# Experts of layer 0: hidden values in two halves with a PSUM bank each, token rows copied by ScalarE and VectorE, and both up-products ahead of both down-products

## The reference

```
logits = x_flat @ W_router
topk_p, topk_i = jax.lax.top_k(jax.nn.softmax(logits, axis=-1), 2)
topk_p = topk_p / topk_p.sum(axis=-1, keepdims=True)
...
for e in range(E):                       # 8 experts, 128 -> 512 -> 128
    h = jax.nn.relu(x_flat @ W1[e] + b1[e])
    out = out + combine[:, e:e + 1] * (h @ W2[e] + b2[e])
```

## Time and profile before

| what | value |
|---|---|
| median of 3 runs | 1411.34 us (1411.24 to 1416.61) |
| the profiled execution's own time | 1410.25 us |
| its span, first to last instruction | 1408.4 us |
| TensorE busy | 1103.4 us, 78% |
| VectorE busy | 825.5 us, 59% |
| ScalarE busy | 744.3 us, 53% |
| GpSimd busy | 546.3 us, 39% |
| experts of layer 0 (first to last residual, line 921) | from 451.3 to 943.2 us |

### The profile page before, as it was taken

How to read it: one execution, slowest core, us unless ns; L and a number is a source line. 1 busy time by engine, 2 the same in 40 slices (tenths; PEclk the granted TensorE clock), 3 DMA queues, 4 the chain that set the end, 5 groups by cost and what they waited for, 6 DMA issues and landing times. The chain is left out here.

```text
span 1408.4 us, 32619 instructions
## 1 busy us (share of the span) xinstructions
PE 1103.4 (78%) x9950; PEld 731.9 (52%) x9951; DVE 825.5 (59%) x1640; ACT 744.3 (53%) x1748; POOL 546.3 (39%) x401
## 2 busy tenths in 40 slices
PE   6869787665602999999999989965999999965586
PEld 2324344332302988888888888862444444422354
DVE  3653345443525555555555555542899999984576
ACT  5855397655711555555555555544666666622364
POOL 0000006555570322322322222232799999991000
PEclk9989899888755999999999999998999999985599
DMA  6100001331122111111111111112111111101000
GB/s 202 47 1 0 1 1 54 112 129 52 33 67 62 44 39 37 38 38 37 37 38 38 38 37 37 38 31 82 30 30 60 60 60 60 46 30 77 0 1 30
DMA packets 60525, 65.22 MB, mean 46 GB/s; under 512 B 9841, under 2 KB 50301, under 8 KB 60336
## 3 DMA queue, kind: packets, MB, share of 16 engines
q1 hardware_dynamic: 49616, 46.47, 11.3%
q0 software_dynamic: 8832, 17.00, 3.7%
q10 hardware_dynamic: 2016, 0.94, 0.2%
HBM read 37.12 MB, written 28.55 MB: 47 GB/s over the span
## 5 line engine op out<-in xcount | busy, mean ns | idle before, releaser
L921 DVE SCALAR_TENSOR_TENSOR m_hl<-ps,m_hh 128x512 f16<-128x512 f32 x292 | 200.4, 686 | 158.2 <-ACT m_hh L893 155.9
L801 POOL DMA_INDIRECT expert_out<-m_result,m_token x148 | 144.5, 976 | 377.8 <-DVE m_result L933 374.1
L893 ACT ACTIVATE m_hh<-ps 128x512 f16<-128x512 f32 x292 | 174.2, 596 | 179.0 <-PE ps L854 176.7
L836 PE MATMUL ps<-m_x,weights 128*128 128x128 f16 x1168 | 212.8, 221 | 44.5 <-ACT m_x L887 43.7
L838 PE MATMUL ps<-m_x,weights 128*128 128x128 f16 x1168 | 211.7, 220 | 0.0
L837 PE MATMUL ps<-m_x,weights 128*128 128x128 f16 x1168 | 211.7, 220 | 0.0
L745 POOL DMA_INDIRECT dispatched<-d_rows,slot x128 | 128.4, 1003 | 211.6 <-DVE slot L647 126.2
L851 PE MATMUL ps<-weights,m_hh 128*128 128x128 f16 x1160 | 209.2, 219 | 0.0
L853 PE MATMUL ps<-weights,m_hl 128*128 128x128 f16 x1160 | 209.2, 219 | 0.0
L852 PE MATMUL ps<-weights,m_hh 128*128 128x128 f16 x1160 | 209.2, 219 | 0.0
L1043 POOL TENSOR_TENSOR iv_pool_sum<-iv_pool_sum,iv_pool_part 128x1024 f32<-128x1024 f32 x80 | 188.6, 2358 | 12.1 <-DVE iv_pool_part L1258 3.8
(11 more groups left out here) (306 smaller groups left out, 2238.0 us busy)
## 6 DMA issues: line engine op xcount, KB each, us to landing
m_rows<-dispatched SPq DMA_DIRECT2D x152, 65.5 KB
X<-x SPq DMA_DIRECT2D x16, 512.0 KB, 4.3
iv_got<-expert_out SPq DMA_DIRECT2D x16, 512.0 KB, 4.3
out<-X SPq DMA_DIRECT2D x16, 512.0 KB, 3.0
Y<-w_moe SPq DMA_DIRECT2D x8, 512.0 KB
expert_out<-m_result,m_token POOLq DMA_INDIRECT x148, 2.2
dispatched<-d_rows,slot POOLq DMA_INDIRECT x128
Y<-w_last SPq DMA_DIRECT2D x1, 2048.0 KB
```

The source lines that it names most:

```text
L801: pool.indirect_dma_start(env.yt, bass.IndirectOffsetOnAxis(ap=token[:, k:k + 1], axis=0), result[:, k, :], None, bounds_check=TOKENS - 1, ...
L836: pe.matmul(out, high, xh, start=True, stop=False)
L893: act.activation(hh[e][:, :], hidden[e], ACT.Relu).then_inc(hi_ready[e], 1)
L921: dve.scalar_tensor_tensor(hl[e][:, :], hidden[e], 0.0, hh[e][:, :], ALU.max, ALU.subtract).then_inc(h_split[e], 1)
```

## The change

- `hidden[e]` becomes two tensors of 256 columns, each in a bank of its own; `high` and `low` become two instructions each, of 256 columns, with a count of their own (`h_ready`, `hi_ready`, `h_split` now count halves). `up` waits for `h_split` twice, at m = 0 and m = 2, and announces each half. `down` announces `y_ready` twice: after its block k = 1, when the first half of `hh[e]` and `hl[e]` is read, and at its end. `down` itself waits for both halves of `h_split`.
- `take` is split: ScalarE copies the high half (127 x 128), VectorE the low half, from a bank each. `up` and `turn_rows` have one more wait (`xl_ready`), and in `up` the product with the low values comes last of the three.
- TensorE's order in a tile becomes `up(i+1, 0)`, `up(i+1, 1)`, `turn_rows(i+2)`, `down(i, 0)`, `down(i, 1)`. ScalarE's: `take(i+2)`, `high(i+1, 0)` twice, `part`, `high(i+1, 1)` twice. VectorE's: `take(i+2)`, four `low`, token copy, `result`.
- The four semaphores of `wait_apart` become one.

The diff, without those of its places that only put `env.passed` for `env.passed["..."]`:

```diff
--- before.py
+++ after.py
@@ -756,7 +756,7 @@
         sem = lambda n: ctx.enter_context(nc.semaphore(n))
         sb = lambda n, s, d=F32: ctx.enter_context(nc.sbuf_tensor(n, s, d))
         landed = [sem(f"m0_landed{k}") for k in range(RING // 2)]
-        rows_ready, turned, x_ready = sem("m0_rows_ready"), sem("m0_turned"), sem("m0_x_ready")
+        rows_ready, turned, x_ready, xl_ready = sem("m0_rows_ready"), sem("m0_turned"), sem("m0_x_ready"), sem("m0_xl_ready")
         h_ready, hi_ready, h_split, y_ready = ([sem(f"m0_{n}{e}") for e in range(2)] for n in ("h_ready", "hi_ready", "h_split", "y_ready"))
         part_ready, out_ready, result_free = (sem(f"m0_{n}") for n in ("part_ready", "out_ready", "result_free"))
         stored, ready = [sem(f"m0_stored{k}") for k in range(OUTS)], sem("m0_ready")
@@ -767,9 +767,10 @@
         xh, xl = x[:, 0, :], x[:, 1, :]
         hh, hl = ([sb(f"m0_{n}{e}", [P, H0], F16) for e in range(2)] for n in ("hh", "hl"))
         part, result, token = sb("m0_part", [P, C]), sb("m0_result", [P, OUTS, C]), sb("m0_token", [P, OUTS], U32)
-        hidden = [env.psum[0][:, e * HALF:(e + 1) * HALF] for e in range(2)]
-        y = [env.psum[1][:, e * HALF:e * HALF + C] for e in range(2)]
-        turn = env.psum[2][:, 0:2 * P]
+        hidden = [[env.psum[e][:, h * HALF:h * HALF + H0 // 2] for h in range(2)] for e in range(2)]
+        y = [env.psum[2][:, e * HALF:e * HALF + C] for e in range(2)]
+        turn = [env.psum[3][:, k * HALF:k * HALF + P] for k in range(2)]
+        part_cols = [slice(h * H0 // 2, (h + 1) * H0 // 2) for h in range(2)]
         at = lambda i: bass.ds(i % RING, 1)
         gate = lambda i, g: rows[:, at(i), C + g:C + g + 1].rearrange("p k c -> p (k c)")
         count = lambda engine, k, low, high: engine.value_load(env.totals[0:1, k:k + 1], min_val=low, max_val=high)
@@ -797,7 +798,7 @@
             pool.sem_inc(result_free, 2)
 
             def send(j, k):
-                wait_apart(pool, out_ready, j * OUTS + k + RING + 1, env.passed["pool"])
+                wait_apart(pool, out_ready, j * OUTS + k + RING + 1, env.passed)
                 pool.indirect_dma_start(env.yt, bass.IndirectOffsetOnAxis(ap=token[:, k:k + 1], axis=0), result[:, k, :], None,
                                         bounds_check=TOKENS - 1, oob_is_err=False).then_inc(stored[k], 16)
                 if k >= 2:
@@ -821,26 +822,31 @@
             def turn_rows(i):
                 pe.wait_ge(rows_ready, i + 1)
                 pe.wait_ge(x_ready, i + 1)
+                pe.wait_ge(xl_ready, i + 1)
                 for part_ in range(2):
-                    mm = pe.matmul(turn[:, part_ * P:(part_ + 1) * P],
+                    mm = pe.matmul(turn[part_],
                                    halves[:, at(i), part_ * C:(part_ + 1) * C].rearrange("p k c -> p (k c)"), idh[:, :], start=True, stop=True)
                 mm.then_inc(turned, 1)
 
             def up(i, e, expert):
                 w = W[:, expert * WCOLS:(expert + 1) * WCOLS]
                 pe.wait_ge(x_ready, i + 2)
-                pe.wait_ge(h_split[e], i + 1)
                 for m in range(KM):
-                    out = hidden[e][:, m * P:(m + 1) * P]
+                    if m % 2 == 0:
+                        pe.wait_ge(h_split[e], i * 2 + m // 2 + 1)
+                    out = hidden[e][m // 2][:, m % 2 * P:(m % 2 + 1) * P]
                     high, low = w[:, m * P:(m + 1) * P], w[:, H0 + m * P:H0 + (m + 1) * P]
                     pe.matmul(out, high, xh, start=True, stop=False)
-                    pe.matmul(out, high, xl, start=False, stop=False)
-                    mm = pe.matmul(out, low, xh, start=False, stop=True)
-                mm.then_inc(h_ready[e], 1)
+                    pe.matmul(out, low, xh, start=False, stop=False)
+                    if m == 0:
+                        pe.wait_ge(xl_ready, i + 2)
+                    mm = pe.matmul(out, high, xl, start=False, stop=True)
+                    if m % 2 == 1:
+                        mm.then_inc(h_ready[e], 1)
 
             def down(i, e, expert):
                 w = W[:, expert * WCOLS:(expert + 1) * WCOLS]
-                pe.wait_ge(h_split[e], i + 2)
+                pe.wait_ge(h_split[e], i * 2 + 4)
                 if e == 0:
                     pe.wait_ge(part_ready, i + 1)
                 else:
@@ -850,14 +856,16 @@
                     high, low = w[:, 2 * H0 + k * P:2 * H0 + (k + 1) * P], w[:, 3 * H0 + k * P:3 * H0 + (k + 1) * P]
                     pe.matmul(y[e], hh[e][:, cols], high, start=(k == 0), stop=False)
                     pe.matmul(y[e], hh[e][:, cols], low, start=False, stop=False)
-                    pe.matmul(y[e], hl[e][:, cols], high, start=False, stop=False)
+                    mm = pe.matmul(y[e], hl[e][:, cols], high, start=False, stop=False)
+                    if k == 1:
+                        mm.then_inc(y_ready[e], 1)
                 pe.matmul(y[e], env.ones16[:, :], w[:, 4 * H0:4 * H0 + C].bitcast(BF16), start=False, stop=True).then_inc(y_ready[e], 1)
 
             def tile(i, pair, following):
                 up(i + 1, 0, following[0])
+                up(i + 1, 1, following[1])
+                turn_rows(i + 2)
                 down(i, 0, pair[0])
-                turn_rows(i + 2)
-                up(i + 1, 1, following[1])
                 down(i, 1, pair[1])
 
             pe.wait_ge(ready, 3)
@@ -883,14 +891,15 @@
             def take(i):
                 act.wait_ge(turned, i + 1)
                 if not isinstance(i, int) or i > 0:
-                    act.wait_ge(h_ready[1], i)
-                act.activation(x[0:C - 1, :, :], turn[0:C - 1, :].rearrange("p (h s) -> p h s", h=2), ACT.Copy).then_inc(x_ready, 1)
+                    act.wait_ge(h_ready[1], i * 2)
+                act.activation(xh[0:C - 1, :], turn[0][0:C - 1, :], ACT.Copy).then_inc(x_ready, 1)
 
             def high(i, e):
-                act.wait_ge(h_ready[e], i + 1)
-                if not isinstance(i, int) or i > 0:
-                    act.wait_ge(y_ready[e], i)
-                act.activation(hh[e][:, :], hidden[e], ACT.Relu).then_inc(hi_ready[e], 1)
+                for h in range(2):
+                    act.wait_ge(h_ready[e], i * 2 + h + 1)
+                    if not isinstance(i, int) or i > 0:
+                        act.wait_ge(y_ready[e], i * 2 - 1 + h)
+                    act.activation(hh[e][:, part_cols[h]], hidden[e][h], ACT.Relu).then_inc(hi_ready[e], 1)
 
             act.wait_ge(ready, 3)
             act.sem_inc(x_ready, 1)
@@ -900,11 +909,11 @@
             take(1)
             total = count(act, 0, PAIRS, MAX_TILES)
             with act.Fori(0, total) as i:
+                take(i + 2)
                 high(i + 1, 0)
-                act.wait_ge(y_ready[0], i + 1)
+                act.wait_ge(y_ready[0], i * 2 + 2)
                 act.wait_ge(out_ready, i + RING)
                 act.activation(part[:, :], y[0], ACT.Copy, scale=gate(i, 0)).then_inc(part_ready, 1)
-                take(i + 2)
                 high(i + 1, 1)
 
         @block.vector
@@ -913,26 +922,41 @@
             dve.memset(x[96:P, 0, :], 1.0).then_inc(ready, 1)
             dve.memset(x[96:P, 1, :], 0.0).then_inc(ready, 1)
             for e in range(2):
-                dve.sem_inc(h_split[e], 1)
+                dve.sem_inc(h_split[e], 2)
             dve.sem_inc(out_ready, RING)
-
-            def low(i, e):
-                dve.wait_ge(hi_ready[e], i + 1)
-                dve.scalar_tensor_tensor(hl[e][:, :], hidden[e], 0.0, hh[e][:, :], ALU.max, ALU.subtract).then_inc(h_split[e], 1)
-
-            low(0, 0)
-            low(0, 1)
+            dve.wait_ge(ready, 3)
+            dve.sem_inc(xl_ready, 1)
+
+            def take(i):
+                dve.wait_ge(turned, i + 1)
+                if not isinstance(i, int) or i > 0:
+                    dve.wait_ge(h_ready[1], i * 2)
+                dve.tensor_copy(xl[0:C - 1, :], turn[1][0:C - 1, :]).then_inc(xl_ready, 1)
+
+            def low(i, e, h):
+                cols = part_cols[h]
+                dve.wait_ge(hi_ready[e], i * 2 + h + 1)
+                dve.scalar_tensor_tensor(hl[e][:, cols], hidden[e][h], 0.0, hh[e][:, cols], ALU.max, ALU.subtract).then_inc(h_split[e], 1)
+
+            take(0)
+            for e in range(2):
+                for h in range(2):
+                    low(0, e, h)
+            take(1)
             total = count(dve, 0, PAIRS, MAX_TILES)
             with dve.Fori(0, total) as i:
-                low(i + 1, 0)
-                dve.wait_ge(y_ready[1], i + 1)
+                take(i + 2)
+                low(i + 1, 0, 0)
+                low(i + 1, 0, 1)
+                low(i + 1, 1, 0)
+                low(i + 1, 1, 1)
+                dve.wait_ge(y_ready[1], i * 2 + 2)
                 dve.wait_ge(part_ready, i + 2)
                 dve.wait_ge(result_free, i + 1)
                 out = bass.ds(i % OUTS, 1)
```

(13 more changed lines are left out.)

## The result

The changed kernel takes 1474.47 us (median of four runs, 1470.47 to 1475.94) against 1411.29 (1410.61 to 1416.61) for the kernel before beside it: ratio 1.0435, 95% interval 1.0402 to 1.0467. The profiled execution took 1475.94, of which 1474.0 are the span.

What follows compares the result with a forecast made beforehand. It took the experts' stage as bounded by TensorE's 2.90 us of products plus a 0.48 wait per step. A held loop of 3.72 against 3.38 over 145 steps gave +49 us: 1460 us, range 1396 to 1481.

Steps and rivals of the forecast that it cites:

- the held loop: Experts' step looping through GpSimd's indirect DMA, ReLU, residual, token copy and `result`: 3.72 us a step, 1460 us, chance 0.65.
- Token copy 0.47 behind the residual: On VectorE, the token copy starts 0.47 us after the last residual's start, between 0.33 and 0.60.
- DMA to ReLU 1.43: ReLU of expert 1's second half starts 1.43 us after the indirect DMA's start, because TensorE's announcement is held.
- z: Cost of TensorE's new waits per step, between 0 and 0.3 us, taken as 0.14; not part of the held loop.
- Halves at 0.38 and 0.42: A 256-column half takes 0.38 us on ScalarE (ReLU) and 0.42 on VectorE (residual).
- Copies at no cost under the downs: Both half copies of the turned rows end before D + 0.7, needed at D + 1.45: cost nothing.
- Step without a hold 3.24 + z: Chain from the downs by ReLU and residual to the `up`s: 3.24 to 3.54 us a step, 3.38 with z = 0.14.
- D: The start of `down(i, 0)` on TensorE, from which the prediction counts times within a step.
- the threshold: TensorE's last down product is free at 0.48 us into the indirect DMA, held from 0.57; expected at 0.66.
- the rivals without a hold: Experts' step with no hold: cheap waits 3.24 to 3.30 us, chance 0.24; dear waits 3.36 to 3.40, chance 0.11.
- the faster case: No hold and cheap TensorE waits: step 3.24 to 3.30 us, time 1391 to 1400 us, chance 0.24.
- so the old wait of 0.48 per step is gone: TensorE's wait for ScalarE's copy of the turned rows before `up`, 0.48 us a step, 70 us in all, disappears.

Runs made afterwards that it cites:

- undisturbed timeline: The changed kernel run again unchanged where nothing was held: 1366.54 us against 1327.89 for the kernel before, ratio 1.0289.
- third session: Four variants run on another chip where holds occur and the kernel before takes 1421.80 us; they took 1478.14, 1496.15, 1435.39 and 1418.89 us.
- second session: Changed kernel again, copy split alone, change in the old order, new order alone, on a chip without holds: ratios 1.0289, 1.0000, 0.9747, 1.0850 to the kernel before.
- two-engine copy: The kernel before with only the turned rows' copy split between ScalarE and VectorE, a bank each: 1327.52 us, ratio 1.0000.
- first trace: Profile of the unchanged kernel before, on which the prediction was based; that execution took 1410.25 us, with a step of 3.378 us.
- `after`: The whole changed kernel, against the kernel before: 1474.47 us, ratio 1.0435, in the main measurement.
- fewer waits: The changed kernel without four TensorE waits that other waits already imply: 1478.14 us, ratio 1.0390 to the kernel before.
- halves alone: The kernel before with only the halves and banks, in its old order and with one copy by ScalarE: 1418.89 us, ratio 0.9990.

## Why the prediction was right

It said 1460 us and a range of 1396 to 1481; the time is 1474. Direction and mechanism are its own, the held loop; the terms:

- *Token copy 0.47 behind the residual (0.33 to 0.60):* measured 0.51.
- *DMA to ReLU 1.43:* 1.47. *ReLU to residual 0.41:* 0.41. *`result` 0.18 and 0.35, then 0.88 to the DMA:* 0.18, and 606.12 to 607.00 = 0.88. The sum is 3.80 instead of 3.72; the typical step of the trace is 3.79. Against the 49 us forecast the loop cost 60, and 5 lie ahead of the stage, which had no term: 16 us, of which 14 are left between the forecast and the median.
- *z = 0.14 and the last product 0.66 into the DMA:* z is 0.11 (605.07 to 606.18 is 1.11, against 1.00 + z), and the product comes at 0.58. "z does not stand in the loop" was tested by itself: with the waits taken out, the step stayed, but for the tile whose DMA is late, where they are worth 0.16.
- *Halves at 0.38 and 0.42:* 383 and 425 ns. The Trainium skill ("ScalarE: Activation LUTs", Rules for kernel authors) budgets some 0.3 us for an activation whose bias is a pointer operand, and 0.83 ns an element, by which a half would take 0.51 (an estimate from that page). These ReLUs are given no bias. The slope holds here (277 ns for the 128 columns of line 895, 383 for 256: 0.83 ns a column), the fixed part is 0.17, and the measurement decides.
- *Copies at no cost under the downs:* so (606.30 and 606.32, ended by 606.61, needed at 607.63). But the gain was booked wrongly, see below.
- *Step without a hold 3.24 + z:* 3.42 in the undisturbed timeline, where 1.58 instead of 1.50 lies between D and the ReLU of expert 1.

Three things in it did not stand up, though none changed the forecast.

First, **the threshold**. The prediction read a fixed phase out of the rows: free at 0.48 into the DMA, held from 0.57. In the third session a product at 0.41 was held, in the second one at 0.68 was not. What is fixed, in tiles with one DMA, is the end of the hold: 1.43 to 1.46 after the DMA's start (medians of four kernels). Where and when it strikes is not a matter of the phase alone. That the hold struck was forecast from this threshold, so this step came true without its reason.

Second, **the rivals without a hold**. They set the changed kernel's free step (3.38 by the estimate) against before's *held* 3.38 and called that even, at a chance of 0.11, and the faster case 0.24. A session without holds frees both kernels, and before is then at 3.17 in its typical step, as its own early stretch showed. The changed kernel is slower there as well, by 2.9%: "slower" did not depend on the hold, as the chances have it.

Third, **"so the old wait of 0.48 per step is gone"** was counted as a saving against which the new chain was set. With the copy split alone, without holds, nothing is saved: the residual of expert 1 behind `result` is waiting right behind it. Under the hold, where this was not run, at most 0.20 of the 0.48 was there to be had: the residual ends at 607.59, `up` of expert 1 starts at 607.94, and 0.15 behind the residual would do. The forecast of the held loop doesn't use the 0.48.

So the order is the cause of the loss: it takes the work out from between a residual and the `up` that needs its bank. Undisturbed that was run by itself and costs 0.77 a step, of which the halves with the split copy return 0.50. Under the hold the ReLU and the residual of expert 1 come to stand in the loop through GpSimd, and the step goes from 3.38 to 3.79; the order alone was not run there, the nearest are the 3.382 and 3.788 with halves in both. That the hold alone makes the difference between 3.45 and 3.79 rests on two traces of the same program and on the tile whose DMA is late (3.37), not on a run that switches it.

## What to carry to other kernels

Where a buffer has one copy, what lies between its release and its next use is its only cover: moving both users together cost 0.77 us a step, and splitting the copy alone brought nothing. Halves with a bank each beat the kernel before in one run only: in the old order, with the split copy, and without holds. Before a wait is costed as a gain, look for the next wait in the same step (here the residual), and compare each rival with the old kernel under the same condition. And where a loop runs through a slow issuer, time saved on an engine outside the loop is handed on to the next wait.

## What was not expected of the hardware

**The same kernel takes 1328, 1411 or 1422 us, depending on the chip or the session.** Between the trace of before and that of the two-engine copy the difference lies only where GpSimd issues indirect DMAs. The stage of the experts took 28 us less (steps of 3.185 against 3.378), and it began 55 us earlier (first `result` at 401.3 against 456.6), though the dispatch ahead of it began with its first indirect DMA at 212.4 and 212.9. Behind it there is no difference: 465.8 us against 465.4 from the last `result` to the end. The stretch from 250 to 300 us, in which the dispatch issues its indirect DMAs, of before in the first trace and of the two-engine copy alone in the second session (these phases are the same code in both; columns as in the earlier trace rows):

```profile
250.00:300.00 50.00, 29.51 (x117) 16.55 (x118) 18.31 (x60) 23.65 (x95) 23.04 (x24) 0.80 0.28 88
```
```profile
250.00:300.00 50.00, 44.45 (x181) 23.45 (x181) 33.00 (x107) 45.26 (x179) 38.24 (x39) 1.00 0.50 158
```

24 indirect DMAs against 39 in the same 50 us, 88 GB/s against 158, and a granted TensorE clock of 0.80, in part its lower level of 1.2 GHz, against 1.00, the upper level throughout. A single indirect DMA takes the same in both (a median of 967 ns for line 745), so what differs is the time between them. Why one chip or session shows both this and the hold, and another neither, stays open; so does what makes the hold strike a given product.

**A hold on TensorE's announcements, as far as it is shown.** In sessions where it occurs, an instruction of ScalarE that waits for TensorE starts some 1.44 us after the start of an indirect DMA if its product comes late in the issue: at 0.69 (before), 0.58 (`after`), 0.41 (fewer waits) and 0.54 (halves alone) into it. VectorE's token copy is late as well, 1.93 after the DMA for a product at 0.93. A product at 0.20 passes (halves alone: 639.90, the copy at 640.16), and so did those at 0.48 in the early stretch of before. The instruction's idle time grows by what the product gains, and in the tile whose DMA is late nothing is held, so the delay is tied to the DMA. Nothing here shows by what means.
